# Four result buffers instead of two in the output stage of a graph layer

## The reference

```python
h = jnp.maximum(_layernorm(x, axis=-1), 0.0)
# in the layer, on h:
edge_in_f = concatenate([h[src], h[dst], edge_features])          # 192 wide
msgs_f = relu(edge_in_f @ W1_f + b1_f) @ W2_f + b2_f              # 128 wide
agg = segment_sum(msgs_f, dst)
# the same with src and dst exchanged and weights _r: msgs_r
agg = agg + segment_sum(msgs_r, src)
node_in = concatenate([agg, h])
out = x + h + (relu(node_in @ Wn1 + bn1) @ Wn2 + bn2)
```

## Time and profile before

| | |
|---|---|
| median of 3 runs | 1609.82 us (1608.27 to 1612.08) |
| the profiled execution's own time | 1610.51 us |
| its span, first to last instruction | 1608.8 us |
| PE busy | 1280.4 us, 80% |
| POOL busy | 1103.2 us, 69% |
| DVE busy | 972.0 us, 60% |
| ACT busy | 942.1 us, 59% |
| last POOL scatter starts | 1334.53 us |
| first transposes of the output stage | 1341.17 us |

### The profile page before, as it was taken

How to read it: one execution, slowest core, us unless ns; L and a number is a source line. 1 busy time by engine, 2 the same in 40 slices (tenths; PEclk the granted TensorE clock), 3 DMA queues, 4 the chain that set the end, 5 groups by cost and what they waited for, 6 DMA issues and landing times.

```text
span 1608.8 us, 29477 instructions
## 1 busy us (share of the span) xinstructions
PE 1280.4 (80%) x7070; PEld 970.6 (60%) x7070; DVE 972.0 (60%) x3294; ACT 942.1 (59%) x2256; POOL 1103.2 (69%) x1003
## 2 busy tenths in 40 slices
PE   5899998457877778887787877778888756899998
PEld 4677777335655555665565656556666544666665
DVE  7999999426666666666666666666666641222222
ACT  4888888345555555555545555555555524677776
POOL 7888888888888888888888888888888761000000
PEclk9999999768788887778778788887777887999999
DMA  6899998425555555555555555555555547999998
GB/s 214 288 312 315 312 316 290 141 51 111 109 111 111 111 105 104 104 105 105 104 104 105 105 102 100 103 103 103 104 102 101 101 71 235 345 353 343 347 342 298
DMA packets 238410, 281.00 MB, mean 175 GB/s; under 512 B 53170, under 2 KB 155200, under 8 KB 238348
## 3 DMA queue, kind: packets, MB, share of 16 engines
q1 hardware_dynamic: 168408, 241.57, 45.2%
q0 software_dynamic: 68992, 38.59, 20.5%
q10 hardware_dynamic: 948, 0.30, 0.1%
HBM read 162.62 MB, written 117.72 MB: 174 GB/s over the span
## 4 chain that ended last, share of the span: by engine, by line
POOL 33%; issue 22%; DMA 15%; PE 4%; DVE 3%; ACT 1%; POOLq 0%; SPq 0%; DVEq 0%; ACTq 0%
POOL table L532 28%; DMA out_x<-ncentred 12%; POOL got_odd L514 6%; DMA table<-to_send,scatter_at 2%; DVE ncentred L1138 2%; DVE same L979 1%; PE bank L833 1%; PE bank L871 1%; DMA same<-table 1%; PE bank L820 1%; PE bank L882 0%; PE bank L818 0%; SPq L392 0%; PE bank L804 0%; PE bank L892 0%
## 5 line engine op out<-in xcount | busy, mean ns | idle before, releaser
L532 POOL DMA_INDIRECT table<-to_send,scatter_at x392 | 622.6, 1588 | 134.0 <-issue 118.4
L846 PEld LDWEIGHTS bank<-message,same 128*128 128x128 f32 x1960 | 270.3, 222 | 44.2 <-issue 39.2
L846 PE MATMUL bank<-message,same 128*128 128x128 f32 x1960 | 290.9, 313 | 4.8 <-DVE message L1011 4.8
L639 ACT ACTIVATE nh<-nx,all_sums,all_rstd 128x64 f32<-128x64 f32 x784 | 280.2, 434 | 0.1
L514 POOL DMA_INDIRECT got_even<-in_x,gather_first x196 | 212.9, 1086 | 39.8 <-issue 34.7
L775 PE MATMUL bank<-wn_h,nturned 128*128 128x256 f32 x784 | 196.7, 394 | 31.7 <-ACT nhidden L683 24.1
L514 POOL DMA_INDIRECT got_odd<-in_x,gather_at x180 | 180.2, 1001 | 54.9 <-issue 54.0
L804 PE MATMUL bank<-ident,h_ends 128*128 128x128 f32 x196 | 52.0, 359 | 198.7 <-DVE h_ends L1020 192.6
L979 DVE TENSOR_SCALAR_CACHE_REDUCE same<-others,ids 128x128 f32<-128x128 int32 (+3 forms) x392 | 190.7, 543 | 12.7 <-issue 7.9
L818 PE MATMUL bank<-turned,w_ends 128*128 128x256 f32 x392 | 167.1, 516 | 37.9 <-ACT turned_edge L609 37.9
L775 PEld LDWEIGHTS bank<-wn_h,nturned 128*128 128x128 f32 x784 | 143.1, 192 | 67.9 <-issue 36.2
(11 more groups left out here) (79 smaller groups left out, 1984.3 us busy)
## 6 DMA issues: line engine op xcount, KB each, us to landing
nx<-in_x SPq DMA_DIRECT2D x194, 256.0 KB
table<-nhidden SPq DMA_DIRECT2D x97, 512.0 KB
same<-table SPq DMA_DIRECT2D x97, 512.0 KB, 5.4
others<-numbers SPq DMA_DIRECT2D x196, 128.0 KB
out_x<-ncentred SPq DMA_DIRECT2D x97, 256.0 KB, 4.4
nx<-out_x SPq DMA_DIRECT2D x55, 256.0 KB, 4.8
out_x<-nh SPq DMA_DIRECT2D x31, 256.0 KB
table<-to_send,scatter_at POOLq DMA_INDIRECT x392
```

The source lines that it names most:

```text
L532: pool.indirect_dma_start(table, bass.IndirectOffsetOnAxis(ap=scatter_at[s][:, k:k + 1], axis=0), to_send[s][:, k, :], None, compute_op=AL ...
L639: last = act.activation(nh[s][:, g, :], nx[place][:, g, :], ACT.Relu, bias=all_sums[:, at, g:g + 1].rearrange("p a g -> p (a g)"), scale=a ...
L846: last = pe.matmul(bank[6 + s][:, k * M:(k + 1) * M], same[s][:, o, k * P:(k + 1) * P], message[s][:, o, :], start=(o == k), stop=(o == KB ...
```

## The change

The results of the output stage go into four buffers in turn: the two of before (`ncentred`) and `nh[0]` and `nh[1]`, tiles of the second stage that the output stage did not use. Each buffer has its own semaphore for its store. DVE, before it writes a result, now waits for the store of the window four before, not two before; the first four windows wait for none. No instruction that computes and no DMA is added or taken away.

```diff
-        nout = ncentred
+        nout = [ncentred[0], ncentred[1], nh[0], nh[1]]
-        n_stored = sems("n_stored")
+        n_stored = [sem(f"n_stored{p}") for p in range(NRING)]
-            def store(i, s):
+            def store(i, s, turn, place):
                 sp.wait_ge(n_out[s], i + 1)
-                store_window(out, i, s, flat(nout[s]), n_stored[s])
+                store_window(out, i, s, flat(nout[place]), n_stored[place])
-                w.do(store, -2)
+                w.do(store, -2, ring=NRING)
-            for s in range(2):
-                sp.wait_ge(n_stored[s], 16 * (NW // 2))
+            for place in range(NRING):
+                sp.wait_ge(n_stored[place], 16 * len(range(place, NW, NRING)))
                 dve.wait_ge(n_back[s], i + 1)
-                if not first(i):
-                    dve.wait_ge(n_stored[s], 16 * i)
-                dve.tensor_tensor(nout[s][:, :, :], bank[6 + s][:, :].rearrange("p (g d) -> p g d", d=D), xh, ALU.add
+                if not first(turn):
+                    dve.wait_ge(n_stored[place], 16 * turn)
+                dve.tensor_tensor(nout[place][:, :, :], bank[6 + s][:, :].rearrange("p (g d) -> p g d", d=D), xh, ALU.add
                                   ).then_inc(n_out[s], 1)
```

## The result

| | before | with the change |
|---|---|---|
| median | 1610.41 us (6 runs, 1607.92 to 1612.22) | 1595.25 us (6 runs, 1590.37 to 1596.58) |
| ratio | | 0.9902, 95% interval 0.9890 to 0.9913 |
| span of the profiled execution | 1608.8 us | 1594.2 us |
| line 871, first to last weight load | 1341.1 to 1599.7 | 1341.1 to 1585.2 |

The kernel is 15 us faster. The forecast was 1604.3 with a range from 1597.0 to 1611.0; the result lies outside it, 0.4 us from the 1594.9 given for the rival "PE becomes the bound". The stage begins at the same time in both profiles and is 14.5 us shorter; all of the gain is there.

A forecast was written before the change was run, and what follows sets the result against it. The prediction took nearly full DMA engines (97% busy) to bound the output stage: profiled 1610.51 us less 5.5 gives 1605.0; that execution lay 0.7 over the median, so 1604.3 us, range 1597 to 1611.

The forecast's parts named there:

- PE becomes the bound: Output stage rival: PE sets the pace, up to 14.9 us less, 1594.9 us; 20%, including cases on the way to it.
- The chain and the 14.9 us: Output stage, 1366 to 1596 us: 81.6% store landing, 12.8% DVE addition; anything but PE costs only 14.9 us.
- DVE is not what ends the stage, so this alone is worth nothing: Output stage additions: without the store wait DVE is up to 1.9 us earlier, by itself worth nothing.
- SP comes earlier: Table loads issued some 3.2 us after transposes of four windows before, leaving 7.2 us; PE never waits at unchanged DMA load.
- up to 1.6 us: Output stage: the held result buffer delays the table loads on SP by this much, 4.84 against 3.22 us.
- What is late next is the DMA engines: Output stage from 1366 us: busy share can only rise from 96.5% to about 99.1%; 5.5 us less taken.
- the row of 331 GB/s at 0.99 from 1350 to 1366 us: Start of the output stage, DVE hardly held: engines at 0.99 moved just 331 GB/s; used against PE as bound.
- The row of 420 GB/s: Two-microsecond stretches moving 420 GB/s; used for PE as bound, since "busy" includes standing still within a packet.
- The wait for the store is mostly a wait for a nearly full set of DMA engines: Output stage stores: median landing 4.5 us, at least 1.5 us of it queueing behind other transfers.
- Full as they are: Output stage rival: spare 3.5% of the DMA engines unusable, landings grow, pace stays 2.676 us, 1609.8 us; 26%.
- dearer transfers: Output stage rival: more in flight slows the engines to 331 GB/s, 10.9 us more, 1620.7 us; 9%.
- Doesn't do what it says: Output stage rival: DVE would still wait for a store, needing landings over 9.5 us; 2%.

The follow-up runs named there:

- e8: Kernel before (two result buffers), with SP issuing the table load of window w+4 ahead of the store of w-2: 1608.34 us, ratio 0.9990.
- e1: Changed kernel with its four buffers, but DVE's addition again waits for the store of two windows before: 1610.49 us, ratio 1.0013 to the kernel before.
- e6: Kernel before, with half the output stage's table transposes, layer 2 matmuls and ReLU left out, all DMAs kept: 1607.70 us, ratio 0.9984.
- e12: Changed kernel with each table load issued one window later on SP: 1636.87 us, ratio 1.0166 to the kernel before.
- e7: Changed kernel, with half the output stage's table transposes, layer 2 matmuls and ReLU left out, all DMAs kept: 1570.35 us, ratio 0.9755 to the kernel before.
- e4: Kernel before without the output stage's loads of x+h: 1593.19 us, ratio 0.9900.
- e3: Kernel before (two result buffers), with the output stage's table loads issued by POOL instead of SP: 1629.75 us, ratio 1.0168.
- e10: Changed kernel, layer 2 with hidden columns as weights, no transposes back, DVE adding the bias too: 1604.32 us, ratio 0.9974 to the kernel before.

## Why the prediction was wrong, point by point

**The chain and the 14.9 us: right.** The chain before was 94% landing and addition, and PE's own pace gave 14.9 us as the most to be had. 14.5 were got.

**"DVE is not what ends the stage, so this alone is worth nothing": wrong.** It held that the late result hurts only through the table loads queued behind it on SP. e8 put these loads ahead and won 1.6 us of 15 (ratio 0.999, an interval that holds 1). The held result also reaches PE through the bank. The loop, whose time the prediction had itself worked out to 2.7 us a window, was the pace (e1, e6).

**SP comes earlier: right**, though the sizes came from one window each. The 3.2 us is 3.53 in the median, so a load has 6.5 us and not 7.2, against landings of up to 6.5, which fits the five short waits, 2.0 us, that are left. The delay by the held buffer was not "up to 1.6 us" but 1.4 in the median (4.89 against 3.53) and over 3 at the longest (7.2). e12 shows that the early issue is needed.

**"What is late next is the DMA engines": this is the step that failed the forecast.** The term was 233 x 0.965 / 0.991, 5.5 us taken, from a busy share read as a fraction of a capacity, 358 GB/s; it held that an earlier issue "does not make a packet faster". The stage became 14.5 us shorter. The rate rose by 6.6% (347 to 370 GB/s) while the share of queue 1 rose by 3% (96.5 to 99.6%), and e7 moved 410 GB/s through the same engines at 103.7%. With the cap gone, PE is next, 14.9 us less, which is the rival given 20%.

Against that rival stood the row of 331 GB/s at 0.99 from 1350 to 1366 us, taken for a ceiling. It is none: PE kept its pace in that stretch, and in the changed kernel the same row is 343 at 1.00, the two rows right behind it 391 and 404 at 1.01 and 1.03, with the same transfers per window. Why a share of 0.99 to 1.00 moved so little in the first 16 us stays open. The row of 420 GB/s was the one to believe, and its share of 1.07 already said that the share is no fraction of a capacity.

Of the two figures of the Trainium skill ("HBM Reference", Specifications (TRN2)), the one for a core that streams alone, about 425 GB/s, is the one that e7's 410 agrees with.

**"The wait for the store is mostly a wait for a nearly full set of DMA engines": wrong in its consequence.** Stores still landed in 4.3 to 4.5 us when 7% more bytes moved per microsecond; only at 410 GB/s did they take 5.0 to 5.2 (e7). With fewer transfers issued just ahead of it a store lands sooner (4.0 us in e4, 2.0 for the last two). That fits a store that stands behind the table and x+h loads issued before it, which is short of saturation; this reading is argued and was not tried by itself.

**The rivals.** "Full as they are" and "dearer transfers" fall with the result, and again with e7. "Doesn't do what it says" falls with the waits after. Of the signs named in advance, the additions' wait for PE and the share of 1.00 came, and the share told nothing; GB/s over 365 with the table's waits gone had been named as the sign of PE as the bound, and it is what came. Landings near 7 us, 25 us of table waits left and 2.61 us a window did not come. The "25 of 39" also added the waits of the weight loads and of the matmuls, which are in part the same pauses.

## What to carry to other kernels

Where a chain of waits closes on itself (landing, addition, issue, landing), work out its time per turn and compare it with the next engine's pace; the gain of one more buffer is the difference, all at once, as soon as the slack covers the longest landing. A busy share of the DMA engines near 1 is no ceiling: look for stretches with more GB/s at the same share before capping a gain by it. A stretch in which nobody waits for DMA does not show the capacity. And take a lead or a delay from all windows and not from one: what must cover it is the longest landing.

## What the runs showed of the hardware that I had not expected

- The DMA share passed 1 (1.04 over 188 us) at 410 GB/s, and stood at 0.97 to 0.98 at 345 to 349 GB/s where two result buffers held the stage (before, e1, e6, e8).
- With the 98 table loads (512 KB, the last 336) issued by POOL instead of SP, each as soon as its buffer was free, the stage went from 2.67 to 2.84 us a window and from 347 to 321 GB/s (e3).
- The f32 matmuls here are two instructions with two weight loads each: 8 calls with 64 moving columns and 128x128 weights are 16 in 1.90 us, some 0.12 us each (e10), and 4 calls with 256 columns are 8 in 1.08 us (before). The transposes of 128 columns are one each, 8 in 0.93 us of pace.
- At 410 GB/s (e7) the rate stayed the same when the bytes per window fell by 7%, and no store landed in under 4.7 us.
